# A two-layer decoder on one core: the experts of a group of sequences are computed between the attention heads of the next group

## What is computed

```python
def reference(x, ctx_1024, ...):
    # layer 0
    # attn : 16 complex heads of 64, rotary phases, decayed keys; logits come from log1p of a
    #        Mahalanobis distance; causal softmax; output projection
    # xattn: 8 heads of an mLSTM cell over the context (log-sigmoid gates, cumulative sums, a
    #        running maximum, exp of differences), layer norm inside
    # ffn  : mixture of experts: a shared expert and the top 2 of 8, each gelu(x w1 + b1) w2 + b2
    # layer 1
    # attn : 16 heads of 8, softmax; xattn: concat(x, mean of the context) W; ffn: top 2 of 8 silu experts
```

## Time and profile before

| | |
|---|---|
| median of 3 runs | 2977.43 us (2976.34 to 2983.9) |
| the profiled execution, its own time | 2985.12 us |
| its span in the trace | 2983.4 us |
| group to group (line 562 of group 0 at 408.1, of group 7 at 2812.0) | 343.4 us |
| second phase, after the loop | 171 us |
| PE, DVE, ACT, POOL busy | 80%, 60%, 36%, 25% |
| mean granted clock of PE | 0.837 of 2.4 GHz |

### The profile page before, as it was taken

How to read it: one execution, slowest core, us unless ns; L and a number is a source line. 1 busy time by engine, 2 the same in 40 slices (tenths; PEclk the granted TensorE clock), 3 DMA queues, 4 the chain that set the end, 5 groups by cost and what they waited for, 6 DMA issues and landing times.

```text
span 2983.4 us, 42978 instructions
## 1 busy us (share of the span) xinstructions
PE 2374.3 (80%) x15312; PEld 1736.1 (58%) x15312; DVE 1791.3 (60%) x3970; ACT 1069.6 (36%) x2714; POOL 749.5 (25%) x637
## 2 busy tenths in 40 slices
PE   3977879786886969788796969878797878969588
PEld 2665647664565646665575636755476655756344
DVE  8965359534886249653795249753595337862554
ACT  2442225432342325423253324523253323533133
POOL 1541025300452005310362005410253004520000
PEclk8987879888887969878798978879798877879699
DMA  4000000000000000000000000000000000010000
GB/s 154 1 1 1 1 23 1 1 1 8 16 1 1 1 23 1 1 1 1 23 1 1 1 23 1 1 1 1 23 1 1 1 3 21 1 63 1 8 14 14
DMA packets 17235, 32.84 MB, mean 11 GB/s; under 512 B 2702, under 2 KB 8854, under 8 KB 16230
## 3 DMA queue, kind: packets, MB, share of 16 engines
q1 hardware_dynamic: 15718, 25.60, 2.5%
q0 software_dynamic: 1280, 4.20, 0.4%
HBM read 23.49 MB, written 5.77 MB: 10 GB/s over the span
## 4 chain that ended last, share of the span: by engine, by line
PE 48%; DVE 34%; issue 11%; ACT 5%; POOL 1%; DVEq 0%; SPq 0%; ACTq 0%; DMA 0%; POOLq 0%
PE bank L844 46%; DVE work L381 8%; DVE work L399 4%; DVE work L390 4%; DVE work L379 3%; ACT work L638 3%; PE bank L848 2%; DVE st L332 2%; DVE act_row L339 1%; DVE max L543 1%; DVE work L548 1%; ACT act_T L638 1%; DVE mv L335 1%; DVE negmax L401 1%; ACT ln_t L638 1%
## 5 line engine op out<-in xcount | busy, mean ns | idle before, releaser
L844 PEld LDWEIGHTS bank<-work 128*128 128x128 f32 (+1 forms) x4128 | 358.4, 215 | 167.9 <-issue 166.6
L844 PE MATMUL bank<-work 128*128 128x128 f32 (+1 forms) x4128 | 379.5, 307 | 64.0 <-DMA work<-in_wo 34.6
L638 ACT ACTIVATE work<-work 128x512 f32<-128x512 f32 (+1 forms) x456 | 271.5, 622 | 395.4 <-DVE work L444 149.8
L638 ACT ACTIVATE work<-bank 128x512 f32<-128x512 f32 x424 | 232.0, 593 | 408.3 <-PE bank L844 380.3
L381 DVE TENSOR_TENSOR work<-bank,table_space 64x512 f32<-64x512 f32 x512 | 352.1, 688 | 6.8
L844 PE MATMUL bank<-sb_cols,work 128*128 128x1 f32 x2048 | 271.7, 262 | 102.0 <-ACT work L638 102.0
L844 PEld LDWEIGHTS bank<-sb_cols,work 128*128 128x128 f32 x2048 | 268.0, 211 | 120.0 <-ACT work L638 119.7
L638 ACT ACTIVATE work<-bank,sb_b_up 128x512 f32<-128x512 f32 x288 | 198.0, 687 | 270.6 <-PE bank L844 265.4
L844 PEld LDWEIGHTS bank<-sb_w_down,work 128*128 128x128 f32 x2304 | 267.3, 192 | 30.6 <-issue 30.6
L519 DVE SCALAR_TENSOR_TENSOR work<-bank,wexp,work 128x128 f32<-128x128 f32 x256 | 72.1, 345 | 353.9 <-PE bank L844 353.9
L844 PE MATMUL bank<-act_T,sb_w_up 128*128 128x512 f32 x576 | 278.1, 631 | 0.0
(11 more groups left out here) (234 smaller groups left out, 3437.6 us busy)
## 6 DMA issues: line engine op xcount, KB each, us to landing
sb_w_up<-in_w_up SPq DMA_DIRECT2D x1, 2304.0 KB
sb_w_down<-in_w_down SPq DMA_DIRECT2D x1, 2304.0 KB
x_T<-in_x_T POOLq DMA_DIRECT2D x8, 256.0 KB, 2.9
x_row<-in_x_row POOLq DMA_DIRECT2D x8, 256.0 KB, 3.0
ctx_T<-in_ctx_T SPq DMA_DIRECT2D x8, 256.0 KB, 2.7
work<-in_ctx_row SPq DMA_DIRECT2D x8, 256.0 KB, 3.4
out<-act_row SPq DMA_DIRECT2D x8, 256.0 KB, 2.3
x_scratch<-act_row SPq DMA_DIRECT2D x7, 256.0 KB, 2.5
```

Source lines behind the costliest of these rows:

```text
L638: return nc.scalar.activation(o, i, f, **k)
L844: return nc.tensor.matmul(o, l, r, start=start, stop=stop, skip_group_check=True)
```

## The change

The loop runs over `G - 1` groups. Ahead of it stand the heads of group 0 alone; an iteration is xattn of group g, then the experts of group g together with the heads of group g+1 (`heads_and_experts`), then attention 1 of group g; behind it xattn, experts alone and attention 1 of the last group. `tally` gives the semaphore counts of heads that are a group ahead. An expert's first products stand in PE's slots 2, 4, ..., 18, its second products in slots 3, 5, ..., 19; its gelus stand at the end of ACT's slots 1, 3, ..., 17; its sum on DVE at the end of slots 3, 5, ..., 19. The shared expert comes last. Banks: the first products now have banks 4 and 5, the second bank 6; scores have bank 3 alone, norms share bank 0 with the queries, transposed probabilities share bank 2 with the values.

```diff
 # ACT
+            def attn0_slot(s, g, d):
...
+                h = s - 4
...
+                        last = fn(P[:, b], rows(wk[12])[:, b], ACT.Exp, bias=negmax[:, h % 2, b:b + 1],
...
+                h = s - 5
...
+                    fn(wk[16 + h % 3][:], bank[2][:], ACT.Copy).then_inc(v_sb, 1)
+                h = s - 1
...
+                    fn(wk[8][:], wk[4 + h % 2][:], ACT.Square)
+                    fn(wk[9][:], wk[6 + h % 2][:], ACT.Square).then_inc(squares, 1)
...
+            def gelus(k, g):
+
+                e = expert(k)
+                for c in range(CH):
+                    act.wait_ge(up, g * E0S * CH + k * CH + c + 1)
+                    if k >= 1:
+                        act.wait_ge(down, g * E0S + k)
+                    fn(hid[c], bank[4 + c % 2][:], ACT.Gelu_apprx_tanh,
+                       bias=res["b_up"][:, e, c:c + 1]).then_inc(gelu, 1)
                 act.preload_act_table_set("natural_log_exp_and_others")
...
+                for s in range(H0 + 6):
...
+                    if heads:
+                        attn0_slot(s, g, 1)
...
+                    if experts and gelu_of(s) is not None:
+                        gelus(gelu_of(s), g)
 # PE
+            def norms_of(h, g, d):
...
+                pe.wait_ge(squares, n(h + 1))
+                pe.wait_ge(q_parts, n(min(h + 2, H0)))
...
+            def queries_of(h, g, d):
...
+                if h > 0:
+                    pe.wait_ge(q_parts, n(h))
+                if h > 1:
+                    pe.wait_ge(norms_sb, n(h - 1))
...
+            def scores_of(h, g, d):
...
+                if h >= 1:
+                    pe.wait_ge(maha, n(h))
...
+            def values_of(h, g, d):
...
+                if h >= 2:
+                    pe.wait_ge(prob_T_sb, n(h - 1))
...
+            def transpose_probs(h, g, d):
...
+                pe.wait_ge(prob, n(h + 1))
+                pe.wait_ge(v_sb, n(min(h + 2, H0)))
...
+            def expert_up(k, c, g):
+
+                if c >= 2:
+                    pe.wait_ge(gelu, g * E0S * CH + k * CH + c - 1)
...
+            def heads_and_experts(g, d, heads, experts):
 
                 for s in range(H0 + 7):
...
+                    up_k = gelu_of(s - 1) if experts else None
+                    down_k = gelu_of(s - 2) if experts else None
+                    if heads and s < H0:
+                        queries_of(s, g, d)
+                        keys_of(s, g, d)
+                    if heads and 0 <= s - 5 < H0:
+                        values_of(s - 5, g, d)
+                    for c in (0, 1):
+                        if up_k is not None:
+                            expert_up(up_k, c, g)
+                        if down_k is not None:
+                            expert_down(down_k, c, g)
+                    if heads and 0 <= s - 2 < H0:
+                        scores_of(s - 2, g, d)
+                    for c in (2, 3):
...
+                    if heads and 0 <= s - 7:
+                        add_head(s - 7, g, d)
...
+                    if heads and 0 <= s - 6 < H0:
+                        transpose_probs(s - 6, g, d)
+                    if heads and 0 <= s - 1 < H0:
+                        norms_of(s - 1, g, d)
...
+            heads_and_experts(0, 0, True, False)
+            with pe.Fori(0, G - 1) as g:
+                xattn(g)
+                pe.wait_ge(in_x, g * 32 + 64)
+                heads_and_experts(g, 1, True, True)
+                attn1_and_tail(g, g + 2)
+            xattn(G - 1)
+            heads_and_experts(G - 1, 1, False, True)
+            attn1_and_tail(G - 1, G)
```

More of the change, by code:

```diff
@@ L358, in top2 @@
                         link(v.scalar_tensor_tensor(t, oh, -4.0, p, ALU.mult, ALU.add))
[L360 to L404, removed]
@@ L405, in _, with attn0_sum, xattn @@
+            def attn0_sum(g, d):
+                dve.wait_ge(head_out, tally(g, d, H0, H0))
+                v.tensor_tensor(resid_a, rows(bank[7]), x_row[:], ALU.add).then_inc(attn_out, 1)
+            def xattn(g):
                 dve.wait_ge(in_ctx, g * 32 + 32)
-                norm(g, 0, resid, act_row[0], done=ln_out)
+                dve.wait_ge(attn_out, g + 1)
+                dve.wait_ge(stored, g * 32 + 16)
+                norm(norm_x, g, 0, resid_a, act_row[0])
                 nabs, e_g, logf, csum_f, a_g, m_g, one = gate
@@ L523, in _, with add_expert @@
-                norm(g, 3, resid, act_row[0], done=ln_out)
+            def add_expert(k, g):
+                dve.wait_ge(down, g * E0S + k + 1)
+                y = rows(bank[6])
+                if k == 0:
+                    dve.wait_ge(rt_w, g + 1)
+                    dve.wait_ge(xb_done, g * 2 + 2)
+                else:
+                    dve.wait_ge(moe_acc, g * E0S + k)
+                if k < E0:
+                    for b in range(GB):
+                        last = v.scalar_tensor_tensor(acc[:, b], y[:, b], wexp[:, b, k:k + 1],
+                                                      (moe_bias if k == 0 else acc)[:, b], ALU.mult, ALU.add)
+                else:
+                    last = v.tensor_tensor(acc[:], y, acc[:], ALU.add)
+                last.then_inc(moe_acc, 1)
@@ new lines, in heads_and_experts @@
+            def heads_and_experts(g, heads, experts):
+                for s in range(H0 + 5):
+                    if heads:
+                        attn0_slot(s, g, 1)
+                    if experts and s == 0:
+                        router_softmax(g)
+                    if experts and s == 1:
+                        router_choice(g)
+                    if experts and gelu_of(s - 2) is not None:
+                        add_expert(gelu_of(s - 2), g)
+                if experts:
+                    dve.wait_ge(moe_acc, g * E0S + E0S)
+                    norm(norm_t, g, 0, acc, act_row[0])
+                if heads:
+                    attn0_sum(g, 1)
@@ L714, in _, with xattn @@
+            def xattn(g):
+                norm(norm_x, g, 0)
+                x_to_T(g, 0, bank[4])
                 act.wait_ge(gate_v, g + 1)
@@ L756, in _ @@
                         fn(prob2[k % 8], ring2[(16 + k) % 6][:], ACT.Exp).then_inc(p2, 1)
-                norm(g, 4)
-                to_T(g, 3, bank[0])
-                norm(g, 5)
-                to_T(g, 4, bank[2])
+                norm(norm_t, g, 1)
+                t_to_T(g, 1, bank[0])
+                norm(norm_t, g, 2)
+                t_to_T(g, 2, bank[2])
+            restart()
+            for s in range(H0 + 6):
+                attn0_slot(s, 0, 0)
+            with act.Fori(0, G - 1) as g:
+                restart()
+                xattn(g)
+                heads_and_experts(g, True, True)
+                attn1_and_tail(g)
+            restart()
+            xattn(G - 1)
+            heads_and_experts(G - 1, False, True)
+            attn1_and_tail(G - 1)
             act.wait_ge(rl_v, G)
@@ new lines, in values_of @@
+            def values_of(h, g, d):
+                n = lambda k: tally(g, d, H0, k)
+                if h >= 2:
+                    pe.wait_ge(prob_T_sb, n(h - 1))
+                if h >= 1:
+                    pe.wait_ge(v_sb, n(h))
+                for b in range(GB):
+                    last = mm(rows(bank[2])[:, b], rows(x_T)[:, b], vo[:, h], start=b == 0)
+                last.then_inc(v_proj, 1)
+            def transpose_probs(h, g, d):
+                n = lambda k: tally(g, d, H0, k)
+                pe.wait_ge(prob, n(h + 1))
+                pe.wait_ge(v_sb, n(min(h + 2, H0)))
+                if h >= 1:
+                    pe.wait_ge(prob_T_sb, n(h))
+                transposes(bank[2], rows(wk[13 + h % 3]), prob_T)
@@ new lines, in add_head @@
+            def add_head(h, g, d):
+                n = lambda k: tally(g, d, H0, k)
+                pe.wait_ge(prob_T_sb, n(h + 1))
+                pe.wait_ge(v_sb, n(h + 1))
+                for b in range(GB):
+                    last = mm(rows(bank[7])[:, b], rows(wk[19 + h % 2])[:, b], rows(wk[16 + h % 3])[:, b],
+                              start=h == 0 and b == 0, stop=h == H0 - 1)
+                last.then_inc(head_out, 1)
+            def expert_up(k, c, g):
+                if c >= 2:
+                    pe.wait_ge(gelu, g * E0S * CH + k * CH + c - 1)
+                elif k > 0:
+                    pe.wait_ge(gelu, g * E0S * CH + k * CH)
+                e = expert(k)
+                mm(bank[4 + c % 2][:], res["w_up"][:, e, c * 128:c * 128 + 128], act_T[:]).then_inc(up, 1)
@@ new lines, in expert_down @@
+            def expert_down(k, c, g):
+                pe.wait_ge(gelu, g * E0S * CH + k * CH + c + 1)
+                if k > 0 and c == 0:
+                    pe.wait_ge(moe_acc, g * E0S + k)
+                e = expert(k)
+                if k == 4 and c == 0:
+                    pe.wait_ge(rt_wT_sb, g + 1)
+                if k == E0 and c == 0:
+                    for b in range(GB):
```

(6 more changed lines are left out.)

546 lines of the change are left out of this document (275 added, 271 removed).

## The result

The changed kernel takes 3397.41 us (median of 4 runs, 3390.74 to 3398.72) against 2980.66 for the kernel before: a ratio of the means of 1.137, interval 1.130 to 1.144. That is slower, as forecast, but by 417 us where 313 were forecast, and 17 us above the top of the range.

What follows compares the result with a forecast made beforehand. PE and DVE were taken as full in the heads, PE in the experts. Seven iterations at +43.7 us (+306) and +7 for group 0's heads gave +313 on 2985.1, 3298, less 7.7: 3290 us; range 3090 to 3380.

Steps and rivals of the forecast that it cites:

- What bounds the kernel now: PE and DVE both full in the heads, PE alone in the experts; so overlapping them can win only little.
- Two slots with an expert in them: An even and an odd slot with one expert: 15.5 + 11.5 = 27.0 us at full clock.
- the chain on ACT: Even slots: gelus and load precede exp, copy and squares, so PE stands about 3.4 us before the transposes, 0.7 before norms.
- the load of gelu's set runs while ACT waits for chunk 0: Even slots: the table load ahead of the gelus lies in ACT's waiting time and is free.
- The clock: Behind PE's gap 3.4 us of full clock lost, taken once a pair: 30.4 us; bounds 27.0 (none) and 33.8 (twice).
- The drain: Slots 16 on, with the last two experts: 43.7 us and 3.4 for the clock, 47.1 in all; before, 45.1.
- The queries' wait: Norms and queries share bank 0, so the next slot's queries start about 0.44 us later, in every slot.
- The sum: One loop iteration 385.3 us, 43.7 more than before; seven give +306, group 0's heads +7, total +313.
- The rule of the Trainium skill on table loads: About 1.38 us of drain on top of each load, 2.66 in all; not counted, would add some 75 us.
- the chain costs more: Rival: clock falls twice a pair, or low clock delays chunk 3 and ACT's chain; 3375 to 3455 us, chance 0.13.
- PE stays fed: Rival: PE's wait for values copy and squares in even slots does not come up; 22.8 us a pair, 2870, chance 0.12.
- the signs that were named: Trace: 9 x 2 loads, PE idle 3 to 4 us before even-slot transposes, even slots near 15, clock 0.85 to 0.9.

Runs made afterwards that it cites:

- the best version: Changed kernel with the gelus moved behind the squares on ACT and the keys projected ahead of the queries: 2848.51 us, ratio 0.957 to the kernel before.
- filler: Changed kernel plus four useless 512-column products on PE in the gap of each even slot: 3285.18 us.
- Experiment 1: Changed kernel with the gelus moved from the end of ACT's odd slot into the even one, behind the squares: 2963.74 us, ratio 0.993 to the kernel before.
- experiment 2: Changed kernel with Square in place of gelu, so the loop has no table loads: 3215.64 us.
- experiment 5: Keys projected ahead of the queries, in four kernels; with experts and heads run one after the other, 3080.24 us against 3127.1 with the queries first.
- the mended order: Changed kernel with the gelus behind the squares on ACT: 2963.74 us; with the keys also ahead of the queries, 2848.51 us.

## Why the prediction was wrong

*What bounds the kernel now*: right. PE and DVE are both full in the heads, and the best version ends with PE 99% busy.

*Two slots with an expert in them*: the chain on ACT was right to 0.1 us where the slot began at full clock (slot 6), and nearly so was the full-clock pair of 27.0 (27.5 with filler at a clock of 0.94). Experiment 1 shows that this chain is what makes the change slow. In one point the steps were wrong: "the load of gelu's set runs while ACT waits for chunk 0". The load itself waited for chunk 0 (1552.56, idle 3.43 on PE). In slots with scores that had no price, as experiment 2 confirms; in slot 18 it cost 1.3 us. Also, the first slots have no values (before slot 5), no transposes (before 6) and no adds (before 7) yet; I charged them in full, 5.3 us an iteration too much on the path.

*The clock*: this is the step that failed, "I take once, by the nearest row: 30.4 us". By my own steps slots 2 to 15 are 7 x 27.0 - 5.3 = 183.7 at full clock; measured were 219.2, so 35.5 / 7 = 5.1 us a pair went to the clock, not 3.4. In place of one fall of 6.8 us there was one of 10, and in some pairs a second. That 219.2 stands near the 212.8 forecast is in part luck: 11.7 us too little for the clock, less the 5.3 too much for the early slots. The drain has the same error: at a clock of 0.85 it lost 0.15 x 56.2 = 8.4 us, where I took 3.4. The upper bound (twice, 6.8) held the value, but only half of that case was taken into the range, so the top of 3380 was too low: the range should have gone up to the 3455 that I had worked out.

*The drain*: 56.2 for 47.1; 5.0 of the 9.1 are the clock. The bias products of the experts (`b_down`, 8 products, 2.07 us at 1.2 GHz) were not in the steps of slot 19, which took 12.3 us instead of 6.5, much of it at 1.2 GHz. Slot 17 took 10.4 for 7.5, again at the lower clock at its start, and slot 18 11.9 for 10, with the 1.3 us behind the load.

*The queries' wait*: right. 0.44 us a slot was forecast, experiment 5 gives 6.8 us for 16.

*The sum*: the iteration came out at 402.8 for 385.3, seven times 17.5, +122. The parts outside the loop took 577 us (3396.9 - 7 x 402.8) where my sum had left 599, -22. Of these, 7 x 1.8 = 12.6 come from taking one group of 341.6 us for all, where the mean is 343.4 (single groups of the old kernel took 335 to 354); the other 9 I have not taken apart. Together +100, from 3298 to 3398.

*The rule of the Trainium skill on table loads* ("ScalarE: Activation LUTs", "What ACT_TABLE_LOAD costs": a drain of 1.38 us on top of each): it would have brought the forecast nearer by 75 us, but for a wrong reason. Gelu starts 0.02 us after its load (1552.56 + 1.28, 1553.86), and exp 0.02 after the other (1557.53 + 1.28, 1558.83), and the second load starts 0.01 behind the gelu ahead of it: no drain here either. Taking that load out moved exp by 1.41 us, not by 2.66.

*The rivals*: "the chain costs more" is what happened, and 3397 lies in its 3375 to 3455; both of its cases occur. In slots 8 and 12 the clock falls a second time, within the even slot's own first products, and chunk 3 comes late: in slot 8 (from 1580.03) the last gelu begins at 1589.77, after 9.74 us where slot 6 has 8.07. In the other pairs it is one fall that lasts longer. "PE stays fed" was priced at 22.8 a pair; it is what the mended order gives, 23.5 and then 22.5, not what the change gives. The changed kernel's trace shows the signs that were named: 9 pairs of loads, the idle time before the transposes, DVE and POOL less busy, and attention 1's first transposes 0.42 us after the norm in place of 4.25. Two signs were off, both by the clock: it is 0.81 over the pairs, not 0.85 to 0.9, and the even slots take 17 to 19 us, not 15.

## What to carry to other kernels

When two stages are interleaved, write down for every engine what stands behind each newly inserted piece in its own queue, and who waits for that: work of the second stage that waits for its input in the middle of a slot belongs behind everything of the first stage that others need in the same slot. Here that choice alone is worth 434 us of 3397. Then price a gap on PE with the low clock behind it, here some 5.1 us of full clock in each pair beside a gap of 3.4 to 4.3. And count small gaps as well: taking a wait of 0.4 us out of every slot saved 51 us beside the large gaps, about its length, and 115 us once those were gone, because the clock then no longer fell.

## What the runs showed of the hardware that was not expected

- The low clock hits the work behind a gap more than the gap: it fell 0.3 us before PE resumed (slot 6) or 0.7 us after (slot 12, where PE resumed at 1659.06), and stayed although PE was full, 10 us at 1.2 GHz behind an idle time of 4.31 us. It also fell for 3.4 us where PE had been idle for 0.36 only.
- Useless products can make a kernel faster: 3285 against 3397 us, with a mean clock of 0.826 for 0.792.
- A table load that the program does not place itself waited for the input of the activation behind it (3.43 us), in the changed kernel; with the gelus behind the squares that wait is nearly gone (18.7 us in all for 81 loads, against 210.9).
- On a clock that no longer falls (0.99), PE executes this kernel's heads and experts at 99% busy, and the whole kernel takes 2849 us, 4.3% less than the kernel before.
